# Projections with their loads in the order of use, masks in four transfers, and the first output's largest values and turned copies elsewhere in VectorE's order

## The reference, cut to what matters

```
xn = layernorm(x)
q  = w8a8_linear(xn, wq, bq)        # rows of xn and rows of wq: divided by max|row|/127, rounded to -127..127
k  = ctx @ wk.T + bk;  v = ctx @ wv.T + bv
s  = q k^T / sqrt(32) + mask;  o = softmax(s) v      # 16 heads
x1 = x + w8a8_linear(o, wo, bo)
h  = silu(layernorm(x1) @ Wg.T) * (layernorm(x1) @ Wu.T)   # W = (integer - 128) * scale
out = x1 + h @ Wd.T
```

## Time and profile before

| | |
|---|---|
| median of 3 runs | 477.53 us (476.21 to 477.82) |
| the profiled execution's own time | 477.79 us |
| its span, first to last instruction | 476.0 us |
| TensorE busy | 465.8 us, 98% |
| VectorE, ScalarE, GpSimd busy | 365.0, 261.9, 238.5 us |
| granted TensorE clock | 1.00 in all slices but for the ends of the table (9 tenths or more) |
| moved by DMA | 77.41 MB, mean 163 GB/s |

### The profile page before, as it was taken

How to read it: one execution, slowest core, us unless ns; L and a number is a source line. 1 busy time by engine, 2 the same in 40 slices (tenths; PEclk the granted TensorE clock), 3 DMA queues, 4 the chain that set the end, 5 groups by cost and what they waited for, 6 DMA issues and landing times.

```text
span 476.0 us, 6950 instructions
## 1 busy us (share of the span) xinstructions
PE 465.8 (98%) x2390; PEld 302.0 (63%) x2390; DVE 365.0 (77%) x486; ACT 261.9 (55%) x465; POOL 238.5 (50%) x131
## 2 busy tenths in 40 slices
PE   8999899999999999999999999999999999999996
PEld 5888588677654454545454454534468778888885
DVE  3589888897988798978879898789966468574325
ACT  3586987321567576666756796667824223222220
POOL 3004211912489888787978878787022122222230
PEclk9999999999999999999999999999999999999999
DMA  5999997998677928091642800030244424446322
GB/s 181 319 313 393 372 280 283 303 275 329 139 197 163 298 72 178 2 211 33 139 106 64 181 2 1 1 133 2 67 154 134 134 78 155 157 133 229 132 68 91
DMA packets 44390, 77.41 MB, mean 163 GB/s; under 512 B 5281, under 2 KB 13505, under 8 KB 44353
## 3 DMA queue, kind: packets, MB, share of 16 engines
q1 hardware_dynamic: 44064, 76.41, 54.3%
q10 hardware_dynamic: 288, 0.52, 0.3%
HBM read 57.95 MB, written 18.87 MB: 161 GB/s over the span
## 4 chain that ended last, share of the span: by engine, by line
PE 77%; DVE 13%; DMA 4%; ACT 3%; issue 2%; SPq 0%; DVEq 0%; ACTq 0%
PE ps L881 13%; PE ps L903 12%; PE ps L853 12%; PE ps L778 8%; PE ps L779 8%; PE ps L990 4%; PE ps L991 4%; PE ps L802 3%; DVE neg_m L1444 3%; PE ps L690 2%; PE ps L692 2%; PE ps L691 2%; DMA raw<-in_ctx_t 2%; PE ps L813 2%; DVE kq_lo L1418 1%
## 5 line engine op out<-in xcount | busy, mean ns | idle before, releaser
L1444 DVE TENSOR_REDUCE neg_m<-ps 128x1 f32<-128x1024 f32 x128 | 149.7, 1216 | 23.4 <-PE ps L853 23.4
L1193 ACT ACTIVATE p_t<-ps 128x512 f32<-128x512 f32 x256 | 137.6, 597 | 43.9 <-PE ps L881 40.4
L1777 POOL TENSOR_TENSOR p_sum<-p_sum,p_t 128x1024 f32<-128x1024 f32 x44 | 105.5, 2410 | 3.2 <-ACT p_t L1193 0.8
L881 PE MATMUL ps<-q_st,k_st 97*128 97x512 f32 x256 | 93.5, 425 | 1.0 <-ACT p_t L1193 0.9
L1777 POOL TENSOR_TENSOR p_sum<-p_t 128x1024 f32<-128x1024 f32 x29 | 70.1, 2419 | 30.0 <-ACT p_t L1193 16.3
L853 PE MATMUL ps<-k_st,q_st 96*128 96x512 f32 x256 | 83.3, 407 | 0.8 <-DVE neg_m L1444 0.4
L881 PEld LDWEIGHTS ps<-q_st,k_st 97*128 97x128 f32 x256 | 47.5, 188 | 51.2 <-ACT p_t L1193 37.3
L778 PE MATMUL ps<-xt_hi,k_st 128*128 128x512 f32 x176 | 68.9, 391 | 0.0
L779 PE MATMUL ps<-xt_lo,k_st 128*128 128x512 f32 x176 | 68.6, 390 | 0.0
L903 PE MATMUL ps<-p_t,v_gr 128*32 128x512 f32 x512 | 68.2, 604 | 0.1
L1721 POOL TENSOR_TENSOR v_st<-v_st,bv_bc 128x512 f32<-128x512 f32 x16 | 20.1, 1286 | 88.8 <-DVE qin L1389 35.0
(11 more groups left out here) (143 smaller groups left out, 664.0 us busy)
## 6 DMA issues: line engine op xcount, KB each, us to landing
k_st<-k_hi_d SPq DMA_DIRECT2D x16, 512.0 KB, 6.9
mask_sb<-in_mask SPq DMA_DIRECT2D x3, 2048.0 KB, 13.2
w_int<-in_w_gate SPq DMA_DIRECT2D x22, 256.0 KB, 2.6
w_int<-in_w_up SPq DMA_DIRECT2D x22, 256.0 KB, 2.9
w_int<-in_w_down SPq DMA_DIRECT2D x22, 256.0 KB, 3.6
k_hi_d<-kq_hi SPq DMA_DIRECT2D x16, 256.0 KB, 6.7
k_lo_d<-kq_lo SPq DMA_DIRECT2D x16, 256.0 KB, 7.4
v_d<-v_st SPq DMA_DIRECT2D x16, 256.0 KB, 10.9
```

Of the source, the lines that this page charges most:

```text
L881: mm = pe.matmul(ps[:, bank, :], k_st[g % SLOTS][0:rows, j, P * lc:P * lc + P], q_st[g % SLOTS][0:rows, j, :], start=True, stop=not with_mask)
L1193: act.activation(p_t[:, q % 4, j, :], ps[:, score_bank(q, j), :], ACT.Exp).then_inc(exp_done, 1)
L1444: dve.tensor_reduce(neg_m[:, g % 2, nt, j:j + 1], ps[:, bank:bank + 2, :], AX_XY, ALU.max, negate=True).then_inc(max_read, 1)
L1777: pool.tensor_tensor(total, former, p_t[:, q % 4, hs, :], ALU.add).then_inc(added_pool, 1)
```

## The change

It has three parts.

**Projections.** SyncE issues all of chunks 0 to 11, then the two small biases, x of batch 0, chunks 12 to 15, wq, x of batch 1 and the four other vectors. The mask comes in four transfers of 128x1024 for each batch, each with its own semaphore, and each of batch 0's waits for its own quarter of the buffer only. The store of V0 is issued ahead of the load of wo. ScalarE takes `centre(0)` and `std(0)` ahead of the last two chunks of item 3 and of `v_tiles(0)`, scales wq after it, and takes `std(1)` after the chunks of item 4. VectorE takes `steps(WQ_SET)` and `round_rows(WQ_SET)` later, `inverse_std(1)` after the scaling of Q0, the low parts of item 5 ahead of the flag, and the copies of T3 ahead of the row of scales S2.

**Largest values of the first output.** Four reductions of 128x512 on VectorE at steps (4,5), (4,6), (4,7) and (5,0) become four of 128x384 at (3,5), (3,6), (3,7) and (4,0), over the columns of groups 0 to 2, and at (4,6) one of 128x4x128 over the columns of group 3 and one of 128x4x2.

**Turned copies.** At step (6,1) VectorE copies the turned rows O ahead of `add` instead of behind it.

```diff
         d_mask = [sem(f"d_mask{b}") for b in range(B)]
+        d_mask_tile = [sem(f"d_mask_tile{t}") for t in range(NT)]
...
-        LARGEST_AT = {(OT, 5): 0, (OT, 6): 1, (OT, 7): 2, (OT + 1, 0): 3}
+        LARGEST_AT = {(OT - 1, 5): 0, (OT - 1, 6): 1, (OT - 1, 7): 2, (OT, 0): 3}
+        LARGEST_OVER = (OT, 6)
...
             def load_mask(b):
-                if b == 0:
-                    sp.wait_ge(mask_seen, NT)
-                sp.dma_start(mask_sb[0][:, :, :],
-                             mask[b].rearrange("(t p) l -> p t l", p=P)).then_inc(d_mask[b], 16)
+                for t in range(NT):
+                    if b == 0:
+                        sp.wait_ge(mask_seen, t + 1)
+                    sp.dma_start(mask_sb[0][:, t, :], mask[b, P * t:P * t + P, :]).then_inc(d_mask_tile[t], 16)
...
             load_mask(1)
+            store_v(0)
             sp.wait_ge(q_rounded, 1)
             sp.dma_start(w_row, wo.rearrange("(t p) c -> p t c", p=P)).then_inc(d_w_row, 16)
-            store_v(0)
...
             kq_tiles("K", 0)
-            scale_set(WQ_SET)
-            split_hi(chunks_of(3))
+            split_hi(chunks_of(3)[:2])
+            centre(0)
+            std(0)
+            split_hi(chunks_of(3)[2:])
             act.wait_ge(d_bias, 4 * 16)
             v_tiles(0)
-            centre(0)
-            std(0)
+            scale_set(WQ_SET)
             scale_set(X_SET)
             kq_tiles("K", 1)
+            split_hi(chunks_of(4))
             std(1)
-            split_hi(chunks_of(4))
...
+            def largest_of_former_groups(t):
+                dve.wait_ge(o_done, OT - 1)
+                dve.tensor_reduce(qmx_parts[:, t, 0:1], o_sb[:, t, 0:C - P], AX_X, ALU.max,
                                   apply_absolute_value=True).then_inc(o_largest, 1)
+            def largest_of_output():
+                dve.wait_ge(o_done, OT)
+                then(dve.tensor_reduce(qmx_parts[:, :, 1], o_sb[:, 0:NT, C - P:C], AX_X, ALU.max,
+                                       apply_absolute_value=True))
+                dve.wait_ge(o_largest, NT)
+                dve.tensor_reduce(qmx[:, O_SET, :], qmx_parts[:, :, :], AX_X, ALU.max).then_inc(o_largest, 1)
...
             round_rows(X_SET + 1, y_a, qb_a[:, 0, :, :], ("T", 0, 3))
+            split_lo(chunks_of(5))
             bank = content(("F", 0, 0))
...
-            split_lo(chunks_of(5))
             round_rows(WO_SET, w_row, qb_a[:, 1, :, :], ("T", 1, 3))
             copy_turned("T", 2, 2, qx_t)
+            copy_turned("T", 3, 3, wo_t)
             scale_row(X_SET + 1, sx_bc)
-            copy_turned("T", 3, 3, wo_t)
...
+                    for key in tail:
+                        if key[1] == "O":
+                            for k, bank in enumerate(ring_banks(key)):
+                                tail_part(0, key[1], key[2] + k, bank)
                     if quad(g, lc) >= 2:
                         add(quad(g, lc) - 2)
```

More of the change, by code:

```diff
@@ L87, in xattn_ffn @@
         qmx = sb("qmx", [P, 6, NT], F32)
+        qmx_parts = sb("qmx_parts", [P, NT, 2], F32)
         qsc = sb("qsc", [P, 6, NT], F32)
@@ L501, in _ @@
             load_chunks(range(0, RAW, 2))
-            load_chunks(range(RAW, 10))
+            load_chunks(range(RAW, 12))
             sp.dma_start(bk_c[:, :], bk).then_inc(d_kq_bias, 16)
             sp.dma_start(bq_c[:, :], bq).then_inc(d_kq_bias, 16)
+            load_x(0)
+            load_chunks(chunks_of(3))
             sp.dma_start(w_row, wq.rearrange("(t p) c -> p t c", p=P)).then_inc(d_w_row, 16)
-            load_chunks(range(10, 12))
-            load_x(0)
+            load_x(1)
             sp.dma_start(bv_bc[:, :], bv.partition_broadcast(P)).then_inc(d_bias, 16)
@@ L1089, in sum_mask @@
             def sum_mask(b):
-                act.wait_ge(d_mask[b], 16)
                 for t in range(NT):
+                    act.wait_ge(d_mask_tile[t], 16 * (B - b))
                     if mask_written[0]:
@@ L1447, in _ @@
             dve.memset(qb_a[:, 0, 0, :], 1.0).then_inc(idle_operands, 1)
-            split_lo(range(10))
-            dve.wait_ge(d_w_row, 16)
-            steps(WQ_SET, w_row)
-            split_lo(range(10, 12))
+            split_lo(range(12))
             dve.wait_ge(d_kq_bias, 2 * 16)
@@ L1454, in _ @@
                 k_tile(0, j)
-            split_lo(chunks_of(3)[:2])
             dve.wait_ge(d_x[0], 16)
@@ L1458, in _ @@
             mean_and_variance(0)
+            split_lo(chunks_of(3)[:2])
+            dve.wait_ge(d_w_row, 16)
+            steps(WQ_SET, w_row)
             split_lo(chunks_of(3)[2:])
-            dve.wait_ge(d_bias, 4 * 16)
-            round_rows(WQ_SET, w_row, qb_a[:, 0, :, :], None)
             inverse_std(0)
             steps_of_rows(0)
+            dve.wait_ge(d_bias, 4 * 16)
             dve.tensor_scalar(swq[:, :], qsc[:, WQ_SET, :], INV_SQRT_D, None, ALU.mult)
@@ L1468, in _ @@
             mean_and_variance(1)
+            round_rows(WQ_SET, w_row, qb_a[:, 0, :, :], None)
             round_rows(X_SET, y_a, qb_a[:, 1, :, :], None)
@@ L1472, in _ @@
             split_lo(chunks_of(4))
-            inverse_std(1)
             copy_turned("T", 0, 0, wq_t)
@@ L1478, in _ @@
                 q_scaled_tile(0, j)
+            inverse_std(1)
             steps_of_rows(1)
@@ L1608, in _ @@
                     for key in tail:
-                        for k, bank in enumerate(ring_banks(key)):
-                            tail_part(0, key[1], key[2] + k, bank)
+                        if key[1] != "O":
+                            for k, bank in enumerate(ring_banks(key)):
+                                tail_part(0, key[1], key[2] + k, bank)
                     if (g, lc) in LARGEST_AT:
-                        dve.wait_ge(o_done, OT)
-                        largest_of_output(LARGEST_AT[g, lc])
+                        largest_of_former_groups(LARGEST_AT[g, lc])
+                    elif (g, lc) == LARGEST_OVER:
+                        largest_of_output()
                     elif (g, lc) == (OT + 1, 1):
@@ L1753, in _ @@
                 if q == LC * (OT + 1) + 1:
-                    pool.wait_ge(o_largest, NT)
+                    pool.wait_ge(o_largest, NT + 1)
                     pool.tensor_scalar(qsc[:, O_SET, :], qmx[:, O_SET, :], 1.0 / QMAX, QUANT_EPS,
```

6 lines of the change are left out of this document (1 added, 5 removed).

## The result

The changed kernel takes 474.92 us (median of 8 runs, 473.39 to 476.01), the kernel before, run beside it, 477.14 (8 runs, 476.13 to 479.29): a ratio of 0.9952, 95% interval 0.9937 to 0.9967. The forecast was 474.2 us, inside 473.2 to 476.3. The profiled execution took 475.19 us with a span of 473.3, against 477.79 and 476.0.

A forecast was written before the change was run, and what follows sets the result against it. TensorE, busy 465.8 of 476.0 us, was taken as the bound. Terms −2.5 − 0.3 + 0.1 − 0.6 = −3.3 us gave execution 474.5, and with the median 0.26 below the profiled execution, 474.2 us; range 473.2 to 476.3.

The forecast's parts named there:

- Up to Q0: Projections: with the chain from x to its reciprocals earlier, Q0 starts near 53.4 instead of 55.90, −2.5 us (1.3 to 2.9).
- T3: Transposes wanting wo's rounded rows: 0.7 to 1.7 us of slack, no cost; rival that T3 waits, 475.4 us, chance 0.17.
- The price on small transfers: Mask loads: eight 0.5 MB pieces instead of two transfers would add up to 12 us if nothing overlapped; trace spoke against it.
- Maxima start: First unit of maxima: T3's copies fill VectorE's wait for S2, so TensorE starts sooner, −0.3 us (bounds 0 and 0.5).
- given back: Rival at the first maxima: q of group 0 lands after 92 behind full DMA engines, time 477.0 us; chance 0.11.
- Largest values: Attention groups 3 and 4: group 3 +0.5, group 4 loses 0.6, last reduction costs 0.25; +0.1 us (−0.2 to +0.7).
- Turned copies: Step (6,1): copies fit while VectorE's add waits for GpSimd, sums start earlier, −0.6 us; bounds no gain and 0.5 loss.
- Sum: Whole kernel: −2.5 − 0.3 + 0.1 − 0.6 = −3.3 us, span 472.7, predicted 474.2 us.

The follow-up runs named there:

- three old and eight new fronts: Traces up to the first scores: old, the kernel before and two runs with only turned copies or only largest values changed; new, eight with the changed projections.
- e6: The changed kernel with each mask again in one 2 MB transfer instead of four: 475.56 us against 476.79 for the kernel before.
- e1: The kernel before with only the projection part of the change: 475.40 us against 476.80 for the kernel before.
- e10: As e9, with the largest values as before the change (four whole tiles in group 4): 473.78 us against 477.01 for the kernel before.
- e12: As e10, with the largest values in the change's form: 473.97 us against 476.74 for the kernel before.
- e8: The kernel before with only chunks 10 and 11 and x(0) ahead of wq in SP's order: 482.28 us against 476.79 for the kernel before.
- e4: The changed kernel with one transfer instead of four for a group's rows of maxima: 473.79 us against 476.80 for the kernel before.
- e5: As e4, with the partial largest values at (3,7), (4,0), (4,1), (4,2): 473.55 us against 476.79 for the kernel before.
- e9: As e5, with group 0's load of v behind its rows of maxima: 473.64 us against 477.01 for the kernel before.

## Why the prediction was right, point by point

**Up to Q0.** Forecast 53.4, measured 53.21; the chain held link by link: wq at 25 to 28 (27.45), reciprocals at about 35.3 (35.35), mask sums to 48.8 (47.9), ScalarE's copies of V1 to 51.1 (50.97), those for Q0 to 53.3 (52.92). The term of −2.5 measured −2.7 between the two profiled executions, but −2.1 between the means of three old and eight new fronts (55.32 and 53.21). Its start, not its end, was off: the execution that it began from had the longest of three stands for wq. The chain laid out for ScalarE has no stand for the vectors; it stood 2.64 us for them, inside slack.

**T3.** No wait; the slack was there as worked out (wo rounded at 78.17, forecast 78.0 to 79). The sums of mask 0 began at 58.08, a second before the forecast, since the pieces were there. The price on small transfers did not show. It was 12 us if nothing overlapped, the prediction's estimate from the 2 us fixed for each DMA that the Trainium skill, "DMA: Bandwidth & Descriptors", gives in the section "Anatomy of one DMA — SWDGE (gpsimd) path", which is about transfers issued by GpSimd; here SyncE issues them. e6, with two transfers instead of eight, is no faster (475.56 and 474.92 us). What the split buys is the time to the first quarter, 2.50 us of ScalarE in e6.

**Maxima start.** −0.3 forecast. From Q0 to the first unit it is 35.93 us now; 36.43, 36.24 and 36.22 in the three old fronts, so −0.3 to −0.5. "Beyond it VectorE and TensorE stay in step, both shifted" is the sentence that failed. The rows of maxima are carried by DMA, and the end of the DMA engines' backlog was not shifted. The missing term is +1.1 at the first scores in the profiled execution, +0.6 in e1's, of which 0.35 is made up in group 0 in each. The rival "given back" had the mechanism, full engines behind a TensorE that moved forward, and looked for it at q of group 0 (where 3 us were left) and not at the next transfer on the way.

**Largest values.** +0.1 forecast, −0.15 in the traces (+0.44 and −0.59), −0.12 between e10 and e12: inside its bounds. The first reductions did delay group 3 as said; the one over the last columns cost less than its 0.25.

**Turned copies.** −0.6 forecast, −0.74 and −0.72 measured, with the mechanism shown twice: VectorE's add ends 1.08 to 1.09 us after GpSimd's whenever it began, so the two copies ahead of it were free. "SBUF — State Buffer" of the Trainium skill, section "Who interferes with whom", has this as an exclusive lock on the shared ports, and both traces agree: the add went from 2.63 us to 1.74 and 1.72 long and still ended 1.1 us behind GpSimd's.

**Sum.** −3.3 forecast; the last matmul is 3.17 us earlier between the profiled executions, by −2.7, −0.5, +0.9 (1.29 us lost between the first maxima and the first scores, 1.08 of them the wait, less the 0.35 made up), −0.15 and −0.7. That the sum fits so well is in part luck: the other four terms came out at −4.1 rather than −3.3, and the wait that was missing took the surplus back. The medians say −2.2. Two things on record go that way: the old fronts' mean was 0.7 us ahead of the one execution at the first scores, and in the profiled pair the last store landed 0.47 later behind TensorE in the changed kernel. That both hold for the other runs is not shown.

## What to carry to other kernels

Before a term is built on a stall for a DMA, ask how it stands in another execution: here three executions of one front took wq up at 18.67 to 19.57 and began Q0 at 54.62 to 55.90, and the one trace at hand was the latest of them. A stand of TensorE can cost more than its length: behind 3.1 us of it in e8 the granted clock was 0.50 for some 3 us, 1.4 us more. When a stage is pulled forward, walk every transfer that is issued inside it, small ones above all, and ask whether the DMA engines are through by the new time; here rows of 2 KB stood behind the megabytes issued before them. The changed kernel with one transfer for the four rows took 473.6 to 474.0 us in five forms (e4, e5, e9, e10, e12), which can't be told from each other: 0.7% below the kernel before rather than 0.5%.
